# A six-part decoder kernel: the order of norm, first keys, triangles and first inverse between the mixture and the delta rule

## The reference, cut to what matters

```python
# part C, per token
logits = flat @ router_w.T;  two best experts by (logits + router_bias), their softmax as weights
hidden = silu(gate_all) * up_all            # 16 experts of 64, and a shared one
x = layernorm(x + sum_k weight_k * hidden_k @ down_k + shared)

# part D, per token t and head (16 heads of 64)
K = K / max(norm(K), 1e-12);  beta = sigmoid(x @ Wbeta + b_beta)
W = W + beta_t * outer(v_t - W k_t, k_t);   o_t = W q_t
x = layernorm(x + concat(o) @ Wout)
```

## Time and profile before

| what | value |
|---|---|
| executions (three) | median 1815.26 us, 1813.98 to 1821.14 |
| the profiled execution | 1819.37 us; its span 1817.6 us |
| TensorE matmul busy | 1552.5 us (85% of the span), 17764 instructions |
| VectorE busy | 1199.5 us (66%) |
| ScalarE busy | 908.2 us (50%) |
| GpSimd busy | 664.2 us (37%) |
| mean granted TensorE clock | 0.946 of full speed |

### The profile page before, as it was taken

How to read it: one execution, slowest core, us unless ns; L and a number is a source line. 1 busy time by engine, 2 the same in 40 slices (tenths; PEclk the granted TensorE clock), 3 DMA queues, 4 the chain that set the end, 5 groups by cost and what they waited for, 6 DMA issues and landing times.

```text
span 1817.6 us, 41185 instructions
## 1 busy us (share of the span) xinstructions
PE 1552.5 (85%) x17764; PEld 801.4 (44%) x17764; DVE 1199.5 (66%) x2325; ACT 908.2 (50%) x1259; POOL 664.2 (37%) x705
## 2 busy tenths in 40 slices
PE   5888877799998999999887788889988999777995
PEld 1222222233334333433423444667777778664442
DVE  6778875777775775767534666666666766465666
ACT  1676664476775775677582132354444543333220
POOL 1010110255564664566471003656755467000000
PEclk9898998899999999999998999899999999887898
DMA  3000002222422222233210100000000001000000
GB/s 145 1 1 1 1 1 79 68 83 71 105 80 68 68 83 68 68 98 90 60 24 14 61 1 1 14 15 15 3 15 15 15 15 35 33 17 0 7 7 12
DMA packets 32406, 70.61 MB, mean 39 GB/s; under 512 B 5328, under 2 KB 7056, under 8 KB 31968
## 3 DMA queue, kind: packets, MB, share of 16 engines
q1 hardware_dynamic: 32224, 67.98, 13.0%
HBM read 47.45 MB, written 20.51 MB: 37 GB/s over the span
## 4 chain that ended last, share of the span: by engine, by line
PE 58%; DVE 29%; ACT 7%; issue 5%; POOL 1%; DMA 1%; SPq 0%; DVEq 0%; ACTq 0%; POOLq 0%
PE ps L159 56%; DVE a_MX L371 4%; DVE b_mx L802 3%; PE ps L221 1%; DVE d_KV L1517 1%; DVE st L165 1%; ACT d_XE L162 1%; DVE sq L200 1%; DVE st L191 1%; DVE b_VL L749 1%; POOL b_EL L874 1%; ACT d_L L162 1%; DVE X L197 1%; DVE c_SG L1302 1%; DVE a_KS L165 1%
## 5 line engine op out<-in xcount | busy, mean ns | idle before, releaser
L874 POOL TENSOR_TENSOR b_EL<-b_X,b_EH 128x1024 f16<-128x1024 f32 x160 | 341.1, 2132 | 310.9 <-ACT b_EH L162 310.9
L802 DVE TENSOR_REDUCE b_mx<-ps 128x2 f32<-128x666 f32 x256 | 217.0, 848 | 100.2 <-PE ps L159 100.0
L1622 POOL TENSOR_TENSOR d_tmp<-d_G,d_XI 128x31 f32<-128x31 f32 (+15 forms) x248 | 128.7, 519 | 291.8 <-DVE d_G L1553 273.0
L856 ACT ACTIVATE b_X<-ps 128x1024 f32<-128x1024 f32 x160 | 163.6, 1023 | 134.5 <-PE ps L159 133.6
L162 ACT ACTIVATE b_EH<-b_X 128x1024 f16<-128x1024 f32 x160 | 169.1, 1057 | 27.9 <-PE ps L159 16.7
L371 DVE TENSOR_REDUCE a_MX<-ps 128x2 f16<-128x1024 f32 x128 | 155.4, 1226 | 39.7 <-PE ps L159 39.5
L408 ACT ACTIVATE a_E<-ps 128x1024 f32<-128x1024 f32 x128 | 131.0, 1024 | 100.2 <-PE ps L159 99.9
L159 PE MATMUL ps<-b_M,b_S 128*128 128x512 f16 (+1 forms) x768 | 177.6, 385 | 2.0 <-ACT b_X L856 1.9
L1625 POOL TENSOR_TENSOR d_XI<-d_XI,d_tmp 128x31 f32<-128x31 f32 (+15 forms) x248 | 140.2, 565 | 19.4
L159 PE MATMUL ps<-b_Hk,b_Hq 64*128 64x333 f16 x512 | 82.7, 320 | 39.9 <-DVE b_mx L802 36.8
L390 POOL TENSOR_TENSOR a_QS<-a_QS,a_MR 128x512 f16<-128x512 f16 x16 | 18.5, 1154 | 256.8 <-ACT a_MR L162 256.8
(11 more groups left out here) (304 smaller groups left out, 3315.5 us busy)
## 6 DMA issues: line engine op xcount, KB each, us to landing
b_S<-s_xk SPq DMA_DIRECT2D x48, 336.0 KB, 6.4
b_M<-s_xq SPq DMA_DIRECT2D x48, 256.0 KB, 5.1
s_xk<-b_Hk SPq DMA_DIRECT2D x16, 336.0 KB, 2.2
s_xk<-b_Lk SPq DMA_DIRECT2D x16, 336.0 KB, 2.5
s_xq<-b_Hq SPq DMA_DIRECT2D x16, 256.0 KB, 2.0
s_xq<-b_Lq SPq DMA_DIRECT2D x16, 256.0 KB, 2.0
d_XI<-eye SPq DMA_DIRECT2D x8, 512.0 KB, 3.6
f_w<-f_w SPq DMA_DIRECT2D x1, 2048.0 KB, 7.8
```

The lines of the kernel that those rows point to most:

```text
L802: v.e.tensor_reduce(out, PS[:, bk:bk + 2, 0:333], AX, ALU.max).then_inc(sem("b_mx"), 1)
L856: a.e.activation(b_X[k % 2], PS[:, bk:bk + 2, :], ACT.Exp, scale=0.125).then_inc(sem("b_ex"), 1)
L874: last = p.e.tensor_tensor(b_EL[k % 6], b_X[k % 2], b_EH[k % 6], ALU.subtract)
L1622: e.tensor_tensor(tm, a, x, ALU.mult).then_inc(*p.step())
```

## The change

Block 0's norm takes three steps of VectorE in each of pairs 2 to 5 of block 1 instead of two in pairs 2 to 7, and its transpose to XT comes at pair 6 instead of pair 8. Keys 0, triangles 0, blocks 0, keys 1 and triangles 1 become one stream, begun behind pair 6 of block 1 instead of behind pair 8: pairs 2 to 8 of block 1, block 2 and block 3 are one stream of 25, and the other has 24 empty steps of 112 ahead. The read-back of inverse 0 moves out of `d_order` to the end of `c_order`, ahead of block 3's down product. In `d_order` the blocks of inverse 1 keep a place in the first weave, behind eight empty steps instead of behind the four steps of that read-back.

In the new order VectorE issues in block 1 the first two sums of squares behind pair 6, the other two, the maximum and the first rsqrt steps behind pair 7, more of rsqrt behind pair 8, the factors and three key multiplies behind pair 0 of block 2 and the fourth behind pair 1; the triangles 0 behind pairs 3 and 4, d_G behind the second of them; keys 1's rsqrt and first multiply behind pairs 5 to 7; triangles 1 behind pairs 3 and 4 of block 3.

```diff
         def c_experts(b, p, route, rest, turned):
-            if b and 1 < p < 8:
-                next(rest, None)
-                next(rest, None)
+            if b and 1 < p < (6 if b == 1 else 8):
+                for _ in range(3 if b == 1 else 2):
+                    next(rest, None)
             if 1 < p < 7:
                 next(route, None)
-            if b and p == 8:
+            if b and p == (6 if b == 1 else 8):
                 turned()
...
-        def c_order(lane, route, experts, tail, rows, turn, last, blocks):
+        def c_order(lane, route, experts, tail, rows, turn, last, blocks, back):
...
-            run(second)
-            weave((both(experts(lane, 2), experts(lane, 3)), 18),
-                  (both(rows(lane, 0), later(6, both(turn(lane, 0), blocks(lane)))), 62),
-                  (later(12, both(rows(lane, 1), later(5, turn(lane, 1)))), 41))
+            keys = both(rows(lane, 0), later(7, both(turn(lane, 0), both(blocks(lane), both(rows(lane, 1), later(16, turn(lane, 1)))))))
+            weave((both(second, both(experts(lane, 2), experts(lane, 3))), 25), (later(24, keys), 112))
+            run(back(lane, 0))
             last(lane, NB - 1)
...
-            weave((last_c(lane), 18), (prep(lane, 0), 17), (both(back(lane, 0), blocks(lane, 1)), 24))
+            weave((last_c(lane), 18), (prep(lane, 0), 17), (later(8, blocks(lane, 1)), 24))
```

More of the change, by code:

```diff
@@ L2386, in _ @@
             c_order(t, c_route_tensor, c_experts_tensor, b_tail_tensor(t), lambda t, m: d_rows_tensor(t, m, ring),
-                    lambda t, m: d_turn_tensor(t, m, ring), c_down_tensor, none)
+                    lambda t, m: d_turn_tensor(t, m, ring), c_down_tensor, none, none)
             d_order(t, d_chain_tensor, d_prep_tensor, lambda t, m: d_keys(t, d_rows_tensor, d_turn_tensor, m, ringD), d_late_tensor, e_first_tensor,
@@ L2401, in _ @@
             c_order(a, c_route_scalar, c_experts_scalar, b_tail_scalar(a), d_rows_scalar, d_turn_scalar, none,
-                    d_first_scalar)
+                    d_first_scalar, d_back_steps_scalar)
             d_order(a, none, d_prep_scalar, lambda a, m: d_keys(a, d_rows_scalar, d_turn_scalar, m), d_late_scalar, e_first_scalar, e_attend_scalar,
@@ L2416, in _ @@
             c_order(v, c_route_vector, c_experts_vector, b_tail_vector(v), d_rows_vector, d_turn_vector,
-                    none, d_first_vector)
+                    none, d_first_vector, d_back_steps_vector)
             d_order(v, d_chain_vector, d_prep_vector, lambda v, m: d_keys(v, d_rows_vector, d_turn_vector, m), d_late_vector, e_first_vector, e_attend_vector,
```

## The result

The changed kernel takes 1822.11 us (median of 20 executions, 1816.81 to 1828.62) where the kernel before takes 1815.24 (20 executions, 1806.89 to 1823.53): ratio 1.0039, 95% interval 1.0025 to 1.0054, that is 7 us slower. The forecast was 1812.2, slightly faster, in a range that ended at 1821; it was wrong. The profiled execution took 1825.27 us, its span is 1823.5, its mean clock 0.942.

What follows compares the result with a forecast made beforehand. Bound: TensorE, VectorE and ScalarE queues in lockstep, with a GpSimd inverse loop behind the join. Only inverse 1's 3.1 us earlier start counted: profiled 1819.37 became 1816.3, median 1815.26 became 1812.2; range 1803 to 1821.

Steps and rivals of the forecast that it cites:

- Later rounds are unchanged: Behind inverse 2: rounds keep their time, so the total moves only by the 3.1 us that inverse 1 starts earlier.
- g: Gain up to block 3's down product: it comes 5.6 us earlier, from the bounds 0 to 10.
- D3: Block 3's down product, at 1149.44 us before; forecast near 1144.
- The sum for block 2: VectorE's time from block 2's pair 1 to its last c_H: 38.8 us against 43.7, 4.9 less.
- D1: Block 1's down product, at 1059.91 us before; forecast 1.7 us late (0 to 3).
- D2: Block 2's down product, at 1113.80 us before; its distance from block 1's was to fall from 53.9 to 49.0 us.
- corner of inverse 0: TensorE's wait at the first inverse's read-back, 3.72 us before; forecast no idle time ahead of it and clock 1.00.
- Rival B: Block 2: GpSimd beside VectorE costs 6 us instead of 3, so the change does nothing, 1815.2 us; chance 0.2.
- rival C: Block 2: TensorE idles over about 6 us in one piece, its clock falls, slower at 1820.8 us; chance 0.15.
- Edit 5: Join of the stages: inverse 1's blocks eight steps later, so it starts 22.3 us after block 3's down product instead of 19.8.
- the loop through GpSimd: Behind the join: VectorE must read back each inverse before the next starts; an inverse takes 38.1 to 38.6 us.
- rival A: Join and first inverses: GpSimd doesn't gate, so the whole 10.8 us are kept, 1804.5 us; chance 0.2.

Runs made afterwards that it cites:

- e5: Changed kernel with TensorE's six-bank ring set to position 3 ahead of the last part, instead of 0; ratio 0.9980 to the kernel before.
- e6: Kernel before with TensorE's six-bank ring set to position 0 ahead of the last part, instead of 3; ratio 1.0039 to the kernel before.
- e3: The changed kernel run again as it is, for a second profile; 1822.89 us, ratio 1.0040 to the kernel before.
- e8: Changed kernel, ring at 3, GpSimd's inverse 0 held until pair 7 of block 2 is multiplied; 1808.76 us, ratio 0.9966 to the kernel before.
- e11: Kernel before with only block 0's norm moved to pairs 2 to 5, ring at 3; 1818.44 us, ratio 1.0019 to the kernel before.
- edit 1: Part of the change: block 0's norm takes three steps per pair over four pairs, its transpose moves from pair 8 to pair 6; alone, ring at 3, ratio 1.0019.
- e10: Changed kernel without the earlier read-back of inverse 0 and the later blocks of inverse 1, ring at 3; 1808.99 us, ratio 0.9961 to the kernel before.
- e12: Kernel before with only the read-back of inverse 0 moved earlier and inverse 1's blocks later; 1815.98 us, ratio 0.9995 to the kernel before.
- e4: Changed kernel with inverse 1's blocks right behind the first read-back, ring at 0; 1810.18 us, ratio 0.9988 to the kernel before.
- e7: Changed kernel with inverse 1's blocks right behind the first read-back and the ring set to 3; ratio 0.9937 to the kernel before.
- e9: Changed kernel, inverse 1's blocks right behind the first read-back, inverse 0 held until block 2's pair 7, ring at 3; 1805.75 us, ratio 0.9935 to before.

## Why the prediction was wrong

Two steps failed. The first is a term that the sum hasn't: "Later rounds are unchanged", and nothing said of part F. The last part took 5.1 us more, and e5 and e6 show that the ring's position makes the difference in the total. The second is g, the gain up to D3: forecast 5.6 us, measured 1.2 in e5 and none in the changed kernel, so that inverse 1, which was to start 3.1 us earlier, starts 0.8 us (e5) or 2.3 us (changed) later than before, counted from D0.

With the ring's position restored the changed kernel stands at 0.9980, 3.6 us under the kernel before (from 7.6 under to 0.5 over); the sum said 3.1. That the two agree is luck: the 3.1 us were inverse 1's earlier start, and there is none. What makes the 3.6, if it isn't chance, is open.

The sum for block 2 also has a slip: its terms (32.5, 2.3, 0.5 and 3) add up to 38.3, not 38.8, which makes D1 to D2 48.5 and g 6.1, further off still. And the bounds of its three terms give g from -1.1 to 12.8 us, not 0 to 10; what was measured lies at the lower end.

| step | forecast | measured (changed kernel or e5) |
|---|---|---|
| D1 late by | 1.7 (0 to 3) | 4.5 (changed), 3.3 (e3, e5) |
| D1 to D2 | 49.0 | 53.0 and 52.6 |
| of it GpSimd beside VectorE | 3 (0 to 6) | 4.5 (e8) |
| D2 to D3 shorter by | 2.4 | 3.3 |
| D3 earlier by | 5.6 (0 to 10) | 1.2 (e5), -0.3 (changed) |
| inverse 1 earlier by, from D0 | 3.1 | -0.8 (e5), -2.3 (changed) |
| inverse 0 starts | 1092.5 | 1096.38 |
| corner of inverse 0 | no wait, clock 1.00 | no wait, clock 1.00 |
| D3 to inverse 1 | 22.3 (before 19.8) | 21.8 |
| VectorE at the second read-back | waits 8.3 (6 to 10) | waits 6.37 |
| read-back to inverse 2, before 15.3 | shorter by up to 2 | 13.2 |
| last part | unchanged | 5.1 more, and 9.8 over e5 |

**D1.** The one-hot came 0.8 us later from D0 on, as reckoned (0.7). What I left out is the clock, which fell behind it: 3.57 us idle instead of 3.49, and a wait of 1.12 just ahead of it where 0.40 was, and TensorE's next gate, up and sel take 3.8 us (e3) instead of 2.1. The row ahead of the one-hot in the kernel before:

```profile
1037.46 1.10 PE L159 MATMUL ps<-XT,c_gt 128*128 128x512 f32 x2 [0.40 <-DVE c_SG L1302]
```

I had argued from the earlier trace rows that 3.49 did no harm; it did none with 0.40 us of idle time ahead of it. e11 shows that edit 1 alone brings both the wait and the low clock; which of the two differences (1.12 for 0.40, 3.57 for 3.49) does it, no run separates. Behind pair 7's silu, which waits for its table, VectorE waited 2.88 us, and D1 waited 1.55 us for its last c_H. ScalarE in the changed kernel:

```profile
1057.44 1.28 ACT L1468 ACT_TABLE_LOAD   x1
1058.73 0.35 ACT L1468 ACTIVATE d_z<-d_z 128x32 f32<-128x32 f32 x2
1059.10 1.28 ACT L1286 ACT_TABLE_LOAD   x1
1060.39 0.60 ACT L1286 ACTIVATE c_SG<-ps 128x512 f32<-128x512 f32 x1
```

Each table load took 1.28 us and the next ACTIVATE began 0.01 us after it; no run shows the drain which the Trainium skill (ScalarE: Activation LUTs, What ACT_TABLE_LOAD costs) adds. D1 was 4.5 us late in one profile, the figure worked out from that page's price, but without a drain in its rows.

**Block 2.** I took 3 us from multiplies that lose 0.2 us each beside GpSimd. The small instructions lose more: in the rows of e5 and e8 0.20 to 0.23 becomes 0.56 to 0.74. Without GpSimd the stretch is still 48.1, not the 46.0 that my sum implies (45.5 by its terms): TensorE's five waits there add up to 7.4 us in e8, the longest 2.46 for c_CT; which of them makes the missing 2.1 was not separated. The Trainium skill (SBUF — State Buffer, Who interferes with whom) says that the later of two such instructions waits out the earlier one. The two-input rows agree: they grow by about 0.45 us, and GpSimd's own instructions take 0.52 and 0.57 us on the mean (part 5 of the changed kernel's profile page). Rival B (contention double, g 2.6) came nearer here than the forecast, and rival C's low clock appeared as well (0.50 in 1108 to 1116), though not by the stop at the d_L copies, behind which TensorE waited only 1.99 us.

**Edit 5.** Right, in place and size: 2.0 us later instead of 2.5, shown by e10, which takes it back (19.85). What I called the loop through GpSimd is borne out: where the second read-back came early it waited for inverse 1, 6.4 us in the changed kernel and 7.65 in e12, and where inverse 1 started early (e4, e7) it didn't wait. A gain of rival A's size (10.8 us) exists, 0.6% in e7, but with that order of work, not this one.

**Last part.** The failed premise is that unchanged program text takes unchanged time. The ring's state crosses the border, and it could have been read before the run: counting the takes of both orders gives 3 and 0.

## What to carry to other kernels

When work is moved between streams that share a ring of buffers, count the ring's position at the end of the changed region as well: it decides which waits the following, untouched stage has, and here it cost 7 to 11 us. Ask of each moved piece what starts it and what stands beside it: beside a chain of small VectorE instructions the first inverse cost 4.5 us, and starting it 12 us later won 3.5 up to D3. And where a loop through a slow engine gates, bring its start forward: that paid here (e7, 0.9937, with e9 the fastest), while moving the work around it did not (e12).

## What was not expected of the hardware

- A VectorE instruction on 64 elements per partition took 0.19 to 0.23 us with GpSimd idle (e8) and mostly 0.53 to 0.74 with GpSimd at work (e5; of the eleven from 1105.55 on, one took 0.22). This holds for TENSOR_SCALAR with one tensor input too (0.20 and 0.60).
- Executions of one kernel lie up to 24 us apart (the kernel before beside e9 to e12: 1804.03 to 1828.01), and of two profiles the one with the lower mean clock can be the longer one though the kernels are equal in their ratios (e7: 1800.3 us at 0.948, e9: 1810.8 at 0.940). The span of one profile against that of another could not have told these variants apart; short pieces between milestones could, and the long piece from D0 to the end of part D could not.
